# A Mamba block with a routed feed-forward: VectorE's multiplication by C moved behind the unit's first other operation

## The chip, the cores and the metric

The kernel runs on one core of one Trainium2 chip. The metric is the device time of one execution in microseconds (us), lower is better. A core has five engines that each run their own instruction queue in order: TensorE (PE), VectorE (DVE), ScalarE (ACT), GpSimd (POOL) and SyncE (SP, here only DMA issues). They wait for each other by semaphores.

## The reference, cut to what matters

Input are 16 rows of 512 positions by 256 features. Each row goes through two halves, each behind a layer norm that is modulated per row: a state space block and a feed-forward with 16 experts, of which each position uses 4.

```
xb = silu(conv3(xn @ W_in[:, :512]));  z = xn @ W_in[:, 512:]
dt = softplus(xb @ W_dt + b_dt);  B = xb @ W_B;  C = xb @ W_C        # 16 states
for t in positions:                                                   # 512 inner channels x 16 states
    h = exp(dt_t * A) * h + (dt_t * x_t) * B_t
    y_t = sum over states of h * C_t
x = x + ga * (residual + ((y + D * xb) * silu(z)) @ W_out)
x = x + gb * experts(layernorm(x) modulated)                          # sigmoid router, top 4 of 16
```

The multiplication by C that the change moves is `h * C_t` of the recurrence, for one state at a time.

## The kernel before

Channels lie on the 128 partitions, in 4 blocks of 128; two blocks make a pair. A **unit** is one state of one pair: 128 x 1024 values (two blocks of 512 positions). A row has 16 states times 2 pairs, 32 units, and the stretch in which a row's 32 units run is called its slot (`NU = 32`). There are 16 slots, so 512 units, and a short tail (`TAIL = 14`). Within a slot the first 6 units are states of pair 0 alone, then the pairs alternate (so two units in a row read the same row of C), and the last 6 are pair 1 alone.

For unit g the engines do this, each in its own queue:

- GpSimd: `drive` multiplies dt*x by B into a slot of the ring `unit` (five slots), two units ahead of VectorE.
- ScalarE: `decay` computes exp(dt * a) twice (one block each) into the PSUM buffer `hbank[g % 2]`. It waits for `c_scaled` of unit g - 2, that is, until the multiplication by C has read that buffer.
- VectorE: `scan` (L765) runs the recurrence in `hbank`. `times_c` (L778) multiplies it by C into the same ring slot, or straight into the sum `gsum` for a pair's first state, and increments `c_scaled`. It waits for the scan's own semaphore and for the row of C.
- GpSimd: `add` (L1375) issues a DMA that adds the ring slot to `gsum`, one unit later.
- SyncE: `load_b` and `load_c` fetch the rows of B and C three units ahead, into rings of four; `load_c` waits for `c_scaled` of the row's last reader.

Everything else is laid beside the units by a fixed plan. A unit has three moments (`part` 0, 1, 2), so a slot has 96. `streams` lists for each slot which work runs between which moments: the norm of the next row, its convolution and silu (VectorE L625, L628, L636), step sizes, gates (L644), the products y times gate (`mix`, L785), the projection of the row before, its statistics, its router (`pick`: six operations, then four, then the rest, L659 to L723) and weights. The experts of the row before run beside both (`Halves`, from moment 38 of a slot to moment 131, that is, into the next one): for each of 16 steps TensorE makes a gate and an up product (L509), ScalarE a tanh (L1103), VectorE two operations (L736, L743), GpSimd one (L1328), and TensorE the down product (L521); twice a row VectorE adds the result (L753, L756). TensorE's products other than `mbank` share three PSUM banks in strict turns. Each engine walks the same plan with its own lag (VectorE two moments, ScalarE one, GpSimd three), so the order of each queue is fixed when the program is written.

On VectorE the walk of a unit is: the scan; in part 0 the experts' step if one is due and then the streams; in part 1 `times_c`, then streams, then experts; in part 2 streams, then experts. Nothing is due in many parts.

Of the kernel before, what the change touches and what calls it, by code (L numbers as in the profile page):

```python
# [47 lines left out]
class Steps:  # L48
# [3 lines left out]
        self.gen, self.steps, self.first, self.final, self.done = gen, steps, first, final, 0  # L52

    def at(self, moment):
        if not self.first <= moment <= self.final:
            return
        upto = (moment - self.first + 1) * self.steps // (self.final - self.first + 1)
        while self.done < upto:
            next(self.gen, None)
            self.done += 1  # L60
        if moment == self.final:
            for _ in self.gen:
                pass


class Halves:
# [3 lines left out]
        self.gen, self.count, self.first, self.final, self.done = gen, count, first, final, 0  # L70

    def at(self, moment):
        while self.done < self.count and self.done * (self.final - self.first) < self.count * (moment - self.first):
            next(self.gen)
            self.done += 1

    def rest(self):
        while self.done < self.count:
            next(self.gen)
            self.done += 1  # L80


def build(nc, d, out):
# [3 lines left out]
    E, I, _ = d["L0_ffn_gate_proj"].shape  # L87
# [7 lines left out]
    NU = 2 * NS  # L95
# [11 lines left out]
    EP = E // 2  # L107
# [3 lines left out]
    ACT_LAG, DVE_LAG, POOL_LAG, SP_LAG = 1, 2, 3, 3  # L111
# [7 lines left out]
    with ctx:  # L119
# [126 lines left out]
        def x1_ready(need, row):  # L246

            for h in range(2):
                t = work.at["proj", row, h]
                need.wait_ge(t.free, t.after)  # L250
# [49 lines left out]
        def xb_at(row, q):  # L300

            return q + DK * (row % 2)
# [35 lines left out]
        def experts_at(older, young, moment):  # L338


            if older:
                older.at(moment + 3 * NU)
            if young:
                young.at(moment)

        def in_columns(dst, src):
            return dst[:, :], d["L0_attn_" + src].rearrange("(k p) -> p k", p=P)
# [269 lines left out]
        def _(eng):  # L617
            need = Passed(eng)

            def silu_inputs(row, pair):  # L620
                for q in (2 * pair, 2 * pair + 1):
                    t, n = work.at["conv", row, q], DK * row + q + 1
                    cv = conv[:, q % 2, :]
                    need.wait_ge(conv_act, n)
                    eng.scalar_tensor_tensor(out=cv[:, 1:T], in0=t.bank[:, 0:T - 1], scalar=conv_w[:, q, 0:1],  # L625
                                             in1=cv[:, 1:T], op0=ALU.mult, op1=ALU.add).then_inc(conv_v, 1)
                    need.wait_ge(conv_v, 2 * n - 1)
                    eng.scalar_tensor_tensor(out=cv[:, 0:T - 1], in0=t.bank[:, 1:T], scalar=conv_w[:, q, 2:3],  # L628
                                             in1=cv[:, 0:T - 1], op0=ALU.mult, op1=ALU.add).then_inc(conv_v, 1)
                    yield  # L630
                    yield
                    need.wait_ge(silu_act, n)
                    if row >= 2:
                        y = work.at["y", row - 2, q]
                        need.wait_ge(y.full, y.after)
                    eng.scalar_tensor_tensor(out=xb[:, xb_at(row, q), :], in0=t.bank[:, :], scalar=1.0, in1=cv, op0=ALU.add,  # L636
                                             op1=ALU.mult).then_inc(t.free, 1)
                    yield

            def gates(row):  # L640
                for q in range(DK):
                    t = work.at["gate", row, q]
                    need.wait_ge(gate_act, DK * row + q + 1)
                    eng.scalar_tensor_tensor(out=gz[:, q, :], in0=gz[:, q, :], scalar=1.0, in1=t.bank[:, :],  # L644
                                             op0=ALU.add, op1=ALU.mult).then_inc(t.free, 1)
                    yield
                    yield

            def pick(row):
# [30 lines left out]
                eng.tensor_reduce(r_g[:, :], r_two[:, :, :], AX.X, ALU.max).then_inc(route_v, 1)  # L680
                eng.tensor_reduce(g_bank, r_two[:, :, :], AX.X, ALU.max).then_inc(route_v, 1)
                at += 1
                yield

                g = r_g[:, :].rearrange("p (t g) -> p t g", g=NGRP)
                this = g.rearrange("p t (g a) -> p t g a", a=1).to_broadcast([P, TT, NGRP, NGRP])
# [13 lines left out]
                    scalar=1.5, in1=members.rearrange("p (t g) m -> p t g m", t=TT), op0=ALU.is_lt,  # L700
                    op1=ALU.mult).then_inc(t.free, 1)
                at -= 1
                yield

                need.wait_ge(t.free, t.after)
                for q in range(TT):
# [16 lines left out]
                eng.tensor_tensor(w_tok[:, :, :], r_w[:, :, 0:E], r_rec[:, :].rearrange(  # L723
                    "p (t a) -> p t a", a=1).to_broadcast([P, TT, E]), ALU.mult).then_inc(route_v, 1)
                assert at + 16 == ROUTE_V * (row + 1)
                yield

            def experts(row):
                for s in range(E + 1):
                    n = E * row + s  # L730
                    a = act[:, n % MOE_RING, :, :].rearrange("p j t -> p (j t)")
                    if s < E:

                        t = work.at["gates2", row, s]
                        need.wait_ge(etanhed, n + 1)
                        eng.scalar_tensor_tensor(out=a, in0=a, scalar=1.0, in1=t.bank[:, :], op0=ALU.add,  # L736
                                                 op1=ALU.mult).then_inc(t.free, 1)
                    yield
                    if s < E:
                        g, t = t, work.at["ups2", row, s]  # L740
                        need.wait_ge(t.full, t.after)
                        need.wait_ge(g.free, g.after)
                        eng.tensor_tensor(a, a, t.bank[:, :], ALU.mult).then_inc(t.free, 1)  # L743
                    yield
                    yield
                    if s in (EP, E):
                        h = s // EP - 1
                        tiles = slice(h * TT // 2, (h + 1) * TT // 2)
                        need.wait_ge(down_done, n)
                        need.wait_ge(gb_in, 16 * (row + 1))  # L750
                        x1_ready(need, row)
                        sums = mbank[:, :].rearrange("p (t h) -> p t h", h=H)
                        eng.tensor_tensor(sums, sums, gb_row[:, :].rearrange("p (a h) -> p a h", a=1).to_broadcast(  # L753
                            [P, TT // 2, H]), ALU.mult).then_inc(moe_v, 1)
                        need.wait_ge(moe_v, 2 * row + h + 1)
                        eng.tensor_tensor(xt[:, row % 2, tiles, :], sums, xt[:, row % 2, tiles, :],  # L756
                                          ALU.add).then_inc(moe_out, 1)
                    yield

            def scan(g):  # L760

                need.wait_ge(driven, g + 1)
                need.wait_ge(decayed, 2 * g + 2)
                h = hbank[g % HB][:, :, :].rearrange("p a t -> p (a t)")
                eng.tensor_tensor_scan(h, h, unit[:, g % RING, :, :].rearrange("p a t -> p (a t)"), 0.0, ALU.mult,  # L765
                                       ALU.add).then_inc(scanned, 1)
# [14 lines left out]
            def mix(row, pair):  # L781
                for q in (2 * pair, 2 * pair + 1):
                    t = work.at["y", row, q]
                    need.wait_ge(t.full, t.after)
                    eng.tensor_tensor(gz[:, q, :], gz[:, q, :], t.bank[:, :], ALU.mult).then_inc(t.free, 1)  # L785
                    yield
                    yield

            def turn_chunks():
                for n, (_, dst, split) in enumerate(chunks):  # L790
                    yield
                    t = work.at["turned", n, 1]
                    o = dst[:, 2:4, :].rearrange("p e h -> p (e h)") if split else dst[:, 2:4, :, :].rearrange(
                        "p e k i -> p (e k i)")
                    need.wait_ge(t.full, t.after)
                    eng.tensor_scalar(o, t.bank[:, :], 0.5 if split else 1.0, None, ALU.mult).then_inc(t.free, 1)
                    yield


            def first_norm():  # L800
# [94 lines left out]
            older = None  # L895
            for slot in range(NB + 1):
                run = slot < NB
                beside = streams(slot, stage_of) if run else last_streams(stage_of)
                young = experts_of(slot - 1, experts) if run else Halves(
                    experts(NB - 1), HALVES, *LAST_EXPERTS_AT)  # L900
                for k in range(NU if run else TAIL):
                    g = slot * NU + k
                    if run:
                        scan(g)
                    for part in range(3):
                        moment = 3 * k + part
                        if part == 0:
                            experts_at(older, young, moment - DVE_LAG)
                        if part == 1 and run:
                            times_c(g)  # L910
                        for s in beside:
                            s.at(moment - DVE_LAG)
                        if part:
                            experts_at(older, young, moment - DVE_LAG)
                older = young
            older.rest()

# [710 lines left out]
```

## Time and profile before

| | |
|---|---|
| median of 3 runs | 2645.66 us (2642.53 to 2646.27) |
| the profiled execution | 2637.64 us, its span 2635.9 us |
| busy: VectorE | 2385.8 us, 91% of the span |
| busy: TensorE (matmul) | 2303.2 us, 87% |
| busy: GpSimd | 2255.9 us, 86% |
| busy: ScalarE | 1489.0 us, 56% |
| first scan, last scan | 55.4 us, 2494.6 us |
| first scans of slots 5, 6, 7, 8 | 803.2, 958.2, 1112.0, 1265.9 us |
| granted TensorE clock | 0.949 of full speed |

Busy shares are averages over stages with different limits, so the rows below are by stage. An instruction's start may lie before the recorded end of the one ahead of it on the same engine: the engine has begun on it while the last results of the other are being written. What an operation takes of a full engine is therefore read from start to start. A bracket at a row's end is idle time of that engine directly before it, and what ended it.

### The profile page before, as it was taken

Reading aid. Unit: us, or ns where it says so; the run is one execution under the profiler, and the core shown is the slowest. Engines: PE = TensorE matmul, PEld = TensorE weight load, DVE = VectorE, ACT = ScalarE, POOL = GpSimd, SP = SyncE. Lnnn points to the kernel's source line nnn. Section 1 sums busy time; section 2 is a strip of 40 time slices with the busy share of each in tenths; the row PEclk is TensorE's granted clock in tenths of the full one; section 3 lists DMA queues with packets and bytes.
Section 4 is the critical chain, followed back from the end, with each engine's and each line's share of the span. In section 5 each row is a group of like instructions: output and inputs, shape, how many; then the busy total and the mean of one; then the engine's idle time right before and its main releaser. Section 6 shows DMA issues by size and latency. Waiting matters only on the chain.

```text
span 2635.9 us, 28145 instructions
## 1 busy us (share of the span) xinstructions
PE 2303.2 (87%) x8814; PEld 1648.3 (63%) x8814; DVE 2385.8 (91%) x2390; ACT 1489.0 (56%) x2825; POOL 2255.9 (86%) x1591
## 2 busy tenths in 40 slices
PE   6356998989989898998989899898989999898799
PEld 2224675756667576666757666575666667576678
DVE  4999999999999999999999999999999999999922
ACT  5656556565655656565565656556565665654320
POOL 2888999998999899899989998999889899988812
PEclk9677999999999999999999999999989999899899
DMA  6998999989999998989999898998989899898911
GB/s 167 256 218 209 216 224 215 235 207 243 214 219 222 210 243 200 248 215 219 222 206 248 192 246 211 224 224 207 249 193 235 209 229 233 200 249 192 233 49 48
DMA packets 312886, 558.72 MB, mean 212 GB/s; under 512 B 46864, under 2 KB 157456, under 8 KB 312736
## 3 DMA queue, kind: packets, MB, share of 16 engines
q0 software_dynamic: 77568, 260.08, 51.2%
q1 hardware_dynamic: 235168, 296.84, 36.9%
q8 instruction: 69, 1.13, 0.2%
q14 instruction: 81, 0.66, 0.1%
HBM read 295.10 MB, written 10.06 MB: 116 GB/s over the span
## 4 chain that ended last, share of the span: by engine, by line
PE 46%; POOL 20%; DVE 13%; issue 9%; ACT 7%; DMA 5%; SPq 0%; POOLq 0%; DVEq 0%
PE wbank L509 17%; PE mbank L521 9%; POOL unit L1361 8%; DVE hbank L765 7%; PE wbank L410 6%; DMA gsum<-unit 4%; PE wbank L451 4%; PE wbank L536 3%; POOL gsum L1375 3%; POOL act L1328 2%; ACT z L939 2%; POOL stat L1249 2%; ACT hbank L1133 2%; PE wbank L435 1%; PE wbank L471 1%
## 5 line engine op out<-in xcount | busy, mean ns | idle before, releaser
L1361 POOL TENSOR_TENSOR unit<-dtx,b_bc 128x1024 f32<-128x1024 f32 x512 | 1417.3, 2790 | 36.5 <-DVE dtx L842 27.9
L765 DVE TENSOR_TENSOR_SCAN hbank<-hbank,unit 128x1024 f32<-128x1024 f32 x512 | 1173.3, 2292 | 50.3 <-ACT hbank L1133 46.6
L1133 ACT ACTIVATE hbank<-dt,a_neg 128x512 f32<-128x512 f32 x1024 | 669.1, 681 | 241.9 <-DVE unit L778 240.0
L1375 POOL DMA_DIRECT2D gsum<-unit x480 | 560.2, 1167 | 73.1 <-DMA gsum<-unit 35.8
L778 DVE TENSOR_TENSOR unit<-hbank,c_bc 128x1024 f32<-128x1024 f32 x480 | 585.4, 1220 | 22.5
L521 PE MATMUL mbank<-down_t,act 128*128 128x256 f32 x2048 | 525.0, 394 | 27.0 <-POOL act L1328 25.9
L509 PE MATMUL wbank<-h_t,up_t 128*128 128x256 f32 x2048 | 509.9, 394 | 37.7 <-DVE xb L636 27.2
L1328 POOL TENSOR_TENSOR act<-act,w_all 128x512 f32<-128x512 f32 x256 | 410.0, 1602 | 142.0 <-DVE act L743 128.2
L509 PE MATMUL wbank<-h_t,gate_t 128*128 128x256 f32 x2048 | 487.3, 381 | 6.3 <-DVE xb L636 5.6
L521 PEld LDWEIGHTS mbank<-down_t,act 128*128 128x128 f32 x2048 | 398.7, 198 | 148.6 <-issue 51.5
L509 PEld LDWEIGHTS wbank<-h_t,up_t 128*128 128x128 f32 x2048 | 397.8, 197 | 141.3 <-DVE xb L636 38.8
L509 PEld LDWEIGHTS wbank<-h_t,gate_t 128*128 128x128 f32 x2048 | 388.0, 190 | 98.0 <-issue 39.0
L1103 ACT ACTIVATE act<-wbank 128x512 f32<-128x512 f32 x256 | 150.6, 588 | 311.4 <-PE wbank L509 311.2
L736 DVE SCALAR_TENSOR_TENSOR act<-act,wbank 128x512 f32<-128x512 f32 x256 | 173.8, 679 | 78.4 <-ACT act L1103 76.9
L410 PE MATMUL wbank<-xb,w_dt 128*128 128x512 f32 x496 | 227.1, 602 | 16.8 <-DVE xb L636 12.7
L743 DVE TENSOR_TENSOR act<-act,wbank 128x512 f32<-128x512 f32 x256 | 174.0, 680 | 13.8 <-PE wbank L509 8.4
L410 PEld LDWEIGHTS wbank<-xb,w_dt 128*128 128x128 f32 x496 | 95.2, 193 | 114.6 <-issue 106.4
L435 PE MATMUL wbank<-xn_t,w_in 128*128 128x512 f32 x256 | 139.9, 675 | 24.3 <-DVE gz L644 21.9
L398 PE MATMUL wbank<-xn_t,w_in 128*128 128x512 f32 x256 | 126.2, 620 | 24.7 <-DVE xb L636 18.1
L536 PE MATMUL wbank<-gsum,ident 128*128 128x512 f32 x256 | 123.8, 607 | 17.2 <-DMA gsum<-unit 17.2
L380 PE MATMUL wbank<-ident,z 128*128 128x128 f32 x256 | 42.4, 306 | 102.7 <-ACT z L939 90.7
L996 ACT ACTIVATE wbank<-z 128x512 f32<-128x512 f32 x60 | 36.1, 602 | 167.1 <-DVE z L628 167.1
(140 smaller groups left out, 2210.8 us busy)
## 6 DMA issues: line engine op xcount, KB each, us to landing
gsum<-unit POOLq DMA_DIRECT2D x480, 512.0 KB, 7.9
b_bc<-bc_scratch SPq DMA_DIRECT2D x352, 256.0 KB, 7.2
c_bc<-bc_scratch SPq DMA_DIRECT2D x352, 256.0 KB, 7.2
w_all<-w_scratch SPq DMA_DIRECT2D x256, 256.0 KB, 4.9
ht<-in_L_attn_x_dram SPq DMA_DIRECT2D x16, 512.0 KB, 6.1
w_out<-in_L_attn_W_out_dram SPq DMA_DIRECT2D x16, 512.0 KB, 8.0
ht<-in_L_attn_x_dram POOLq DMA_DIRECT2D x16, 512.0 KB, 8.0
out_dram<-xt SPq DMA_DIRECT2D x16, 512.0 KB, 3.1
```

What stands on the lines that cost most here:

```text
L410: m = eng.matmul(t.bank[:, :], w_dt[:, k, m_ * P:(m_ + 1) * P], xb[:, xb_at(row, k), :], start=k == 0, stop=k == DK - 1)
L509: m = eng.matmul(t.bank[:, j * HT:(j + 1) * HT], w[:, 2 * first + j, k, :], h2_t[:, row % 2, k, h * HT:(h + 1) * HT], start=k == 0, stop=k ...
L521: m = eng.matmul(mbank[:, u * H:(u + 1) * H], act[:, (n - 1) % MOE_RING, j, u * P:(u + 1) * P], down_t[:, e, :], start=(e == 0 and u == 0) ...
L536: m = eng.matmul(t.bank[:, :], ident[:, :], gsum[:, (2 * p + k) % SUMS, a, :], start=k == 1, stop=k == 0)
L736: eng.scalar_tensor_tensor(out=a, in0=a, scalar=1.0, in1=t.bank[:, :], op0=ALU.add, op1=ALU.mult).then_inc(t.free, 1)
L743: eng.tensor_tensor(a, a, t.bank[:, :], ALU.mult).then_inc(t.free, 1)
L765: eng.tensor_tensor_scan(h, h, unit[:, g % RING, :, :].rearrange("p a t -> p (a t)"), 0.0, ALU.mult, ALU.add).then_inc(scanned, 1)
L778: eng.tensor_tensor(o, hbank[g % HB][:, :, :], c_bc[:, s:s + 1, :].to_broadcast([P, 2, T]), ALU.mult).then_inc(c_scaled, 1)
L1133: eng.activation(hbank[g % HB][:, a, :], dt[:, 2 * q + a, :], ACT.Exp, scale=a_neg[:, 2 * q + a, n:n + 1]).then_inc(decayed, 1)
L1328: eng.tensor_tensor(a, a, w_all[:, n % W_RING, :, :], ALU.mult).then_inc(weighted, 1)
L1361: eng.tensor_tensor(unit[:, g % RING, :, :], dtx[:, 2 * q:2 * q + 2, :], b_bc[:, s:s + 1, :].to_broadcast([P, 2, T]), ALU.mult).then_inc(d ...
L1375: eng.dma_start(gsum[:, 2 * pair + k, :, :], unit[:, g % RING, :, :], accum_op=ALU.add).then_inc(summed[pair][k], 16)
```

## The change

Each step of a stream on VectorE now says how many operations it made, and the walk of a unit keeps `times_c` back until one was made, at the latest until the end of the unit. `times_c` stands behind the first part that made something. Where part 0 made something, the queue is as before; where nothing else is due in the unit, too. No operation is added or removed, and the other engines' queues are the same.

```diff
 class Steps:
     def at(self, moment):
+        made = 0
         if not self.first <= moment <= self.final:
-            return
+            return made
         upto = (moment - self.first + 1) * self.steps // (self.final - self.first + 1)
         while self.done < upto:
-            next(self.gen, None)
+            made += next(self.gen, None) or 0
             self.done += 1
         if moment == self.final:
-            for _ in self.gen:
-                pass
+            for more in self.gen:
+                made += more or 0
+        return made
...
@@ def experts (VectorE)
-                    yield
+                    yield int(s < E)
...
@@ the walk of a slot on VectorE
                     if run:
                         scan(g)
+                    due = run
                     for part in range(3):
-                        moment = 3 * k + part
+                        moment, made = 3 * k + part, 0
                         if part == 0:
-                            experts_at(older, young, moment - DVE_LAG)
-                        if part == 1 and run:
+                            made += experts_at(older, young, moment - DVE_LAG)
+                        for s in beside:
+                            made += s.at(moment - DVE_LAG)
+                        if part:
+                            made += experts_at(older, young, moment - DVE_LAG)
+                        if due and (made or part == 2):
                             times_c(g)
-                        for s in beside:
-                            s.at(moment - DVE_LAG)
-                        if part:
-                            experts_at(older, young, moment - DVE_LAG)
+                            due = False
```

The other yields of VectorE's streams change in the same way (`yield 2` behind the two convolution taps, `yield 1` behind a silu, gate, mix or copy, `yield 6`, `4` and `7` in `pick`, `2 * int(s in (EP, E))` behind the experts' sums), and `Halves.at` and `experts_at` pass the number on.

## Rows read from the trace of the kernel before

**Rows 1.** Busy time by window: us, PE, PEld, DVE, ACT, POOL, clock, DMA
```profile
996.00:1060.00 64.00, 50.03 (x202) 34.96 (x201) 60.18 (x76) 44.38 (x105) 59.33 (x46) 0.97 0.85 205
1060.00:1148.00 88.00, 88.00 (x339) 64.51 (x338) 85.59 (x73) 48.21 (x72) 80.52 (x54) 0.98 0.99 236
```

**Rows 2.** Timeline of TensorE: start us, us, engine, line, operation, shapes [idle before]
```profile
1059.54 3.48 PE L509 MATMUL wbank<-h_t,up_t 128*128 128x256 f32 x8 [1.95 <-DVE xb L636]
```

**Rows 3.** Timeline at the end of that stretch, ScalarE and VectorE
```profile
1149.75 0.38 ACT L1045 ACTIVATE xt<-wbank 128x256 f32<-128x256 f32 x1 [3.64 <-PE wbank L454]
...
1151.88 2.30 DVE L765 TENSOR_TENSOR_SCAN hbank<-hbank,unit 128x1024 f32<-128x1024 f32 x1 [1.09 <-ACT hbank L1133]
```

**Rows 4.** Timeline of VectorE, two units (k=25 and 26 of slot 6)
```profile
1079.95 2.29 DVE L765 TENSOR_TENSOR_SCAN hbank<-hbank,unit 128x1024 f32<-128x1024 f32 x1
1082.15 0.67 DVE L743 TENSOR_TENSOR act<-act,wbank 128x512 f32<-128x512 f32 x1
1082.74 1.21 DVE L778 TENSOR_TENSOR unit<-hbank,c_bc 128x1024 f32<-128x1024 f32 x1
1083.86 2.29 DVE L765 TENSOR_TENSOR_SCAN hbank<-hbank,unit 128x1024 f32<-128x1024 f32 x1
1086.26 1.23 DVE L778 TENSOR_TENSOR unit<-hbank,c_bc 128x1024 f32<-128x1024 f32 x1
1087.40 0.68 DVE L736 SCALAR_TENSOR_TENSOR act<-act,wbank 128x512 f32<-128x512 f32 x1
1088.18 0.69 DVE L743 TENSOR_TENSOR act<-act,wbank 128x512 f32<-128x512 f32 x1
```

**Rows 5.** Router at k=11: slot 6 (VectorE, ScalarE), slot 5, and its waits in all
```profile
1006.36 2.29 DVE L765 TENSOR_TENSOR_SCAN hbank<-hbank,unit 128x1024 f32<-128x1024 f32 x1
1008.68 1.23 DVE L778 TENSOR_TENSOR unit<-hbank,c_bc 128x1024 f32<-128x1024 f32 x1
1009.82 0.22 DVE L659 SCALAR_TENSOR_TENSOR r_ch<-wbank,choice_bias 128x64 f32<-128x64 f32 x1
...
1010.87 0.25 DVE L681 TENSOR_REDUCE wbank<-r_two 128x16 f32<-128x96 f32 x1
1011.15 0.23 DVE L690 TENSOR_TENSOR wbank<-wbank,r_g 128x64 f32<-128x64 f32 x1
...
1009.04 0.22 ACT L1084 ACTIVATE r_s<-wbank 128x64 f32<-128x64 f32 x1
...
855.92 0.23 DVE L659 SCALAR_TENSOR_TENSOR r_ch<-wbank,choice_bias 128x64 f32<-128x64 f32 x1 [1.02 <-ACT r_s L1084]
...
DVE r_ch L659 <- ACT r_s L1084: 9.6, 7, 3.3
```

**Rows 6.** GpSimd's sum behind k=12's multiplication: slot 6, slot 4
```profile
1020.01 0.93 POOL L1375 DMA_DIRECT2D gsum<-unit  x1 [0.28 <-DVE unit L778]
...
711.36 0.91 POOL L1375 DMA_DIRECT2D gsum<-unit  x1
```

**Rows 7.** The scan of k=17, slot 6
```profile
1038.68 2.30 DVE L765 TENSOR_TENSOR_SCAN hbank<-hbank,unit 128x1024 f32<-128x1024 f32 x1 [0.81 <-ACT hbank L1133]
```

**Rows 8.** The scan of k=15, slot 0
```profile
119.10 2.30 DVE L765 TENSOR_TENSOR_SCAN hbank<-hbank,unit 128x1024 f32<-128x1024 f32 x1 [1.70 <-ACT hbank L1133]
```

**Rows 9.** GpSimd's last sum, behind the last unit
```profile
2498.66 0.86 POOL L1375 DMA_DIRECT2D gsum<-unit  x1 [1.75 <-DVE unit L778]
```

**Rows 10.** Around k=3 of slot 7: VectorE, ScalarE, the scan of k=5
```profile
1124.22 2.29 DVE L765 TENSOR_TENSOR_SCAN hbank<-hbank,unit 128x1024 f32<-128x1024 f32 x1
1126.61 1.23 DVE L778 TENSOR_TENSOR unit<-hbank,c_bc 128x1024 f32<-128x1024 f32 x1
...
1127.32 0.60 ACT L1103 ACTIVATE act<-wbank 128x512 f32<-128x512 f32 x1 [3.60 <-PE wbank L509]
1127.82 2.52 ACT L1133 ACTIVATE hbank<-dt,a_neg 128x512 f32<-128x512 f32 x4
...
1133.73 2.29 DVE L765 TENSOR_TENSOR_SCAN hbank<-hbank,unit 128x1024 f32<-128x1024 f32 x1
```

More of the change, by code:

```diff
@@ L72, in at @@
     def at(self, moment):
+        made = 0
         while self.done < self.count and self.done * (self.final - self.first) < self.count * (moment - self.first):
-            next(self.gen)
+            made += next(self.gen) or 0
             self.done += 1
+        return made
     def rest(self):
@@ L338, in experts_at @@
         def experts_at(older, young, moment):
+            made = 0
             if older:
-                older.at(moment + 3 * NU)
+                made += older.at(moment + 3 * NU)
             if young:
-                young.at(moment)
+                made += young.at(moment)
+            return made
         def in_columns(dst, src):
@@ L629, in silu_inputs @@
                                              in1=cv[:, 0:T - 1], op0=ALU.mult, op1=ALU.add).then_inc(conv_v, 1)
-                    yield
+                    yield 2
                     yield
@@ L637, in silu_inputs @@
                                              op1=ALU.mult).then_inc(t.free, 1)
-                    yield
+                    yield 1
             def gates(row):
@@ L645, in gates @@
                                              op0=ALU.add, op1=ALU.mult).then_inc(t.free, 1)
-                    yield
+                    yield 1
                     yield
@@ L682, in pick @@
                 at += 1
-                yield
+                yield 6
                 g = r_g[:, :].rearrange("p (t g) -> p t g", g=NGRP)
@@ L702, in pick @@
                 at -= 1
-                yield
+                yield 4
                 need.wait_ge(t.free, t.after)
@@ L725, in pick @@
                 assert at + 16 == ROUTE_V * (row + 1)
-                yield
+                yield 7
             def experts(row):
@@ L737, in experts @@
                                                  op1=ALU.mult).then_inc(t.free, 1)
-                    yield
+                    yield int(s < E)
                     if s < E:
@@ L743, in experts @@
                         eng.tensor_tensor(a, a, t.bank[:, :], ALU.mult).then_inc(t.free, 1)
-                    yield
+                    yield int(s < E)
                     yield
@@ L757, in experts @@
                                           ALU.add).then_inc(moe_out, 1)
-                    yield
+                    yield 2 * int(s in (EP, E))
             def scan(g):
@@ L785, in mix @@
                     eng.tensor_tensor(gz[:, q, :], gz[:, q, :], t.bank[:, :], ALU.mult).then_inc(t.free, 1)
-                    yield
+                    yield 1
                     yield
@@ L796, in turn_chunks @@
                     eng.tensor_scalar(o, t.bank[:, :], 0.5 if split else 1.0, None, ALU.mult).then_inc(t.free, 1)
-                    yield
+                    yield 1
             def first_norm():
```

## The prediction

> **What bounds the kernel now.** The table of busy shares names no bound (VectorE 91%, TensorE 87%, GpSimd 86%), so I read by stage. One slot (a row's 32 units) lasts about 154 us, and slots 2 to 14, counted from 0, repeat each other closely; I use slot 6 and the start of slot 7 (1112.0), with k for a unit's place in its slot. The busy time by window splits 152 us in two: in the 64 us from k=9 to k=20 TensorE has 14 us idle, in the 88 us after them none, while VectorE is idle 2.4 us there [rows 1]. TensorE's timeline shows where that stretch starts, behind the convolution's last step on VectorE [rows 2]; at its end ScalarE waits 3.64 us for the projection, and the next scan 1.09 us for ScalarE [rows 3]. So from k=21 to k=8 of the next slot TensorE sets the pace; before that it is a chain through ScalarE, VectorE and GpSimd.
>
> **What VectorE gains.** I worked the plan's arithmetic (steps and halves by moment, lag 2) through for all 512 units. In 241 another operation stands ahead of the multiplication already, in 112 the unit has no other, and in 159 the multiplication moves: ten a slot in slots 2 to 14, at k=0, 1, 3, 5, 11, 13, 15, 24, 26, 31. The timeline prices it [rows 4]: an independent operation starts 2.20 us after its scan (1079.95 to 1082.15), the multiplication 2.40 us after it (1083.86 to 1086.26), and 2.32 where it is the second reader of its C row (1006.36 to 1008.68 in [rows 5]). An independent follower comes 0.59 us behind a 0.67 us operation, whether it is the multiplication (1082.15 to 1082.74) or not, and 1.12 to 1.14 us behind a multiplication. So a move saves 0.12 or, mostly, 0.19 to 0.20 us; over the 159 (50 and 109 times) that is 27 us. In 44 units it also comes between an expert's two operations, whose start-to-start is 0.78 us back to back (1087.40 to 1088.18) against 0.59: 8 us more. In all 35 us of VectorE time, 1.3%. The edit adds no instruction and no new pair of engines to wait on each other.
>
> [...]
>
> **Where the gain goes.** Seven of the ten places (24, 26, 31, 0, 1, 3, 5) lie in the stretch in which TensorE has no gap. What VectorE wins there becomes a longer wait for ScalarE ahead of the scan of k=9: worth 0. Places 13 and 15 lie between the multiplication of k=12 and the scan of k=17. There GpSimd runs without a gap from the sum it issues at 1020.01, waiting 0.28 us for the multiplication of k=12 [rows 6], through the norm of the next row, and the scan of k=17 then waits 0.81 us for ScalarE behind that [rows 7]. Also 0.
>
> **What the move costs.** At k=11 the first other operations are the router's six. They need ScalarE's scores, written from 1009.04 to 1009.26, while the scan is through for a follower at 1006.36 + 2.20 = 1008.56. Today the multiplication (1008.68 to 1009.82) covers that gap, and in other slots not all of it: the router's first operation waits in 7 cases, 9.6 us together, 1.02 of them in slot 5 [rows 5]. In the new order VectorE stands still until about 1009.30; the six go by, and the multiplication's 1.14 us comes behind them, less 0.11 as the pair 1010.87 to 1011.15 (0.28 apart) loses its dependent step (0.17): 1.03 us later if the scores already were the last to come. Here the router starts 0.52 us sooner than today, so 0.51 is left. The rest of the router, the scan of k=12 and its multiplication follow without a gap. Reading the same rows in 15 slots gives 0.51 to 0.69 us in seven (2, 3, 6, 7, 10, 14, 15) and 1.03 in eight.
>
> How much of it passes? GpSimd issues the sum 5.62 us after the scan of k=12 when VectorE is last; where its own chain is later the loss is covered. In the slots that start at 1.03, GpSimd is later by 1.13 us in slots 4, 11 and 12 (711.36 without a wait, [rows 6]), 1.0 in 8, 0.5 in 1 and 13, 0.1 in 5 and 0 in 9. With the six uncovered small ones of slots 2 to 14 (0.51, 0.54, 0.51, 0.63, 0.69, 0.51) the sum over slots 1 to 14 is 0.5 + 0.03 + 0.93 + 1.03 + 0.5 + 3.4 = 6.4 us. Behind it lie the scan of k=17 and a VectorE without a free place up to TensorE's restart, so it ends up in the span.
>
> The ends. Slot 0 has no experts. Moves at k=3, 4, 7, 8 and 11 save 0.9 us ahead of the wait at k=15 (1.70 us for ScalarE [rows 8]); ScalarE and GpSimd are paced by the multiplications there, so I take all of it, with bounds 0 and -1.4 (all eight moves). In slot 15 the router costs 0.5 and 13 and 15 give back 0.2 before GpSimd takes over. In the last unit of all the multiplication stands 0.39 us later (2.20 + 0.59 against 2.40), and GpSimd's last sum waits for it [rows 9]; k=26 gives 0.36 back. Together +0.3. Sum: 6.4 - 0.9 + 0.3 = +5.8 us.
>
> **The lateness itself.** Behind a moved multiplication wait ScalarE's two decays for the scan two units on, GpSimd's sum (and the slot of the ring behind it) and SyncE's load of a C row; nothing else is moved past a queue. The longest delay is k=3: the scan at 1124.22, then a mix and an expert's operation whose tanh ends at 1127.92, then the multiplication, at 1128.55 in place of 1126.61. Its signal comes about 1129.8; ScalarE's decays for k=5 then end near 1131.2 in place of 1130.3, and the scan that needs them starts at 1133.73 [rows 10]. Slack 2.5 us, cost 0; in the other places the delay is 0.4 to 1.8 us. If an activation fell in between, the bound is the 1.9 us of lateness in each of 13 slots: 25 us.
>
> **Result.** The profiled execution took 2637.64 us (span 2635.9), so 2643.4 is expected of it; the median of the runs shown is 8.0 us above it, and the same +5.8 there gives 2651.5. A measurement of this kernel tells about 0.2% (5.3 us) from no change, and the forecast sits on that edge. I call the likeliest case slower, with its own range +1 to +11: the low end has half the slots covered and slot 0 at its best, the high end has none covered (7 times about 0.57 and 8 times 1.03, 12 us).
>
> **Rivals.**
> - VectorE bounds throughout and the 35 us come back, less 12 us at the router: -23 us, about 2623. For it: in the first window VectorE is the busiest, 60.2 of 64 us [rows 1]. Against: TensorE has no gap for 88 us, and VectorE waits at its end. A weaker form, in which a third passes (-8), belongs here. Chance 0.12.
> - All absorbed: the router's scores often come later than shown, or GpSimd's chain does, and the cost hides as in slots 4, 8, 11 and 12: within 3 us. Chance 0.28.
> - The delayed multiplication reaches ScalarE's queue: a decay held by it stands ahead of an expert's tanh, TensorE gets its bank back late and loses its gapless stretch. It decides from 2.5 us of lateness at k=3; price 1 to 1.9 us in 13 slots: +13 to +25 on top, about 2670. Chance 0.10.
> - An operation between scan and multiplication saves VectorE nothing: the 0.9 us of slot 0, the 0.5 us of slot 15 and the 0.11 at each router fall away, so about +9 us, 2654. The pairs of 2.20 and 2.40 us [rows 4] leave it 0.02. [...]
>
> The forecast has 0.48, of which 0.28 lies above the edge and 0.20 below; of the absorbed case 0.02 is faster, the rest within. So faster 0.12 + 0.02 = 0.14, same 0.20 + 0.26 = 0.46, slower 0.28 + 0.10 + 0.02 = 0.40. The range takes in forecast and absorbed case, the weak form of the first rival and the start of the third: 2638 to 2663.
>
> **What the profile after would show.** In ten places a slot the multiplication starts 2.79 us or more after its scan; the idle time ahead of the router's first operation grows to some 0.7 us in every slot and up to 2.2 where it waits today; ahead of the scan of k=9 it grows from 1.09 by up to the 1.9 us won before it; from k=12 to k=17 nothing changes; slots like 6 get 0.5 us longer. I am wrong if the scan of k=9 no longer waits for ScalarE (VectorE was the bound), if TensorE shows idle time after k=22, or if the scan of k=5 begins to wait.

## The result and the profile after

The change makes the kernel slower by 0.42%: ratio of the times after to before 1.0042, 95% interval 1.0030 to 1.0054 (about 11 us). The medians of six runs each, 2653.57 and 2645.66 us, lie 7.9 us (0.30%) apart, at the low end of that interval. The profiled execution of the changed kernel has a span of 2651.8 us, 15.9 above the one before, which was 8.0 us faster than its kernel's median; so the two traces show more than the typical loss. All ratios compare executions in the chip's ordinary state: one of 7047.88 us (the added operation at k=12) and one of 3411.16 us (the kernel before) are outside it. The forecast was 2651.5 us and +0.22%: right in direction and in the place of the loss, and about half of the measured ratio.

The page after, its busy line and three of its groups (line engine op, operands, count | busy, mean ns | idle before, releaser). In the changed file the scan is L771, the multiplication by C L784, the decay L1141, the experts' first operation L742.

```profile
PE 2313.2 (87%) x8814; PEld 1660.8 (63%) x8814; DVE 2367.7 (89%) x2390; ACT 1492.9 (56%) x2825; POOL 2255.9 (85%) x1591
...
L771 DVE TENSOR_TENSOR_SCAN hbank<-hbank,unit 128x1024 f32<-128x1024 f32 x512 | 1172.9, 2291 | 41.6 <-ACT hbank L1141 39.1
L784 DVE TENSOR_TENSOR unit<-hbank,c_bc 128x1024 f32<-128x1024 f32 x480 | 583.7, 1216 | 10.9
L742 DVE SCALAR_TENSOR_TENSOR act<-act,wbank 128x512 f32<-128x512 f32 x256 | 174.1, 680 | 113.1 <-ACT act L1111 111.5
```

VectorE is busy 18 us less than before (2385.8). What it saved is found again as waiting: the experts' first operation now waits 111.5 us for ScalarE's tanh in all, where the page of before has 76.9:

```profile
L736 DVE SCALAR_TENSOR_TENSOR act<-act,wbank 128x512 f32<-128x512 f32 x256 | 173.8, 679 | 78.4 <-ACT act L1103 76.9
```

The rest of the saving is idle time: 22.5 us ahead of the multiplication became 10.9, and 13.8 ahead of the experts' second operation became 8.0. With the 18 us that makes 35.5, the 35 us of the prediction. Against it stand the 34.6 us more ahead of the experts' first operation and 8.7 less ahead of the scans (50.3 to 41.6), so about three quarters of the saving are found again in these two rows. The loss is in another row, VectorE's waits for the router's scores (engine, result, line, waited for: us in total, times, longest):

```profile
DVE r_ch L665 <- ACT r_s L1092: 34.0, 16, 3.5
```

It was 9.6 us in 7 cases [rows 5]. Here is the router at k=11 of slot 6, the timeline of VectorE (start us, us, ...), with ScalarE's scores and TensorE's logits beside it:

```profile
1011.95 2.29 DVE L771 TENSOR_TENSOR_SCAN hbank<-hbank,unit 128x1024 f32<-128x1024 f32 x1
1016.53 0.23 DVE L665 SCALAR_TENSOR_TENSOR r_ch<-wbank,choice_bias 128x64 f32<-128x64 f32 x1 [2.30 <-ACT r_s L1092]
...
1017.59 0.25 DVE L687 TENSOR_REDUCE wbank<-r_two 128x16 f32<-128x96 f32 x1
1017.75 1.21 DVE L784 TENSOR_TENSOR unit<-hbank,c_bc 128x1024 f32<-128x1024 f32 x1
1018.88 0.22 DVE L696 TENSOR_TENSOR wbank<-wbank,r_g 128x64 f32<-128x64 f32 x1
...
1016.28 0.22 ACT L1092 ACTIVATE r_s<-wbank 128x64 f32<-128x64 f32 x1
...
1012.43 3.57 PE L477 MATMUL wbank<-router_t,h_t 128*128 128x16 f32 x16 [1.50 <-ACT h_t L1081]
```

The order is the forecast one: the scan, six operations, the multiplication 0.16 us behind the sixth and 1.13 us wide. The wait is 2.30 us, not 0.7; over slots 2 to 15 it is 0.92 to 2.30. The scores came late, because the 16 small matrix products of the logits took 3.57 us, and the windows show why (us, then busy time by engine, granted clock, DMA):

```profile
1006.00:1011.00 5.00, 3.47 (x20) 2.63 (x18) 4.82 (x5) 4.58 (x10) 4.82 (x5) 1.00 0.64 141
1011.00:1013.00 2.00, 0.56 (x3) 0.60 (x4) 2.00 (x2) 1.29 (x2) 2.00 (x3) 0.78 0.28 84
1013.00:1017.00 4.00, 4.00 (x18) 3.82 (x18) 1.67 (x3) 0.93 (x3) 4.00 (x3) 0.50 0.95 237
```

TensorE had the full clock (2.4 GHz) until about 1012.1, was busy for only 0.56 of the 2 us from 1011 to 1013, and worked at half (1.2 GHz) through the logits. In slot 6 of the kernel before it was as idle ahead of the logits, and the clock fell as well, but only 1.8 us after their start, so that they took 1.93 us:

```profile
1005.00:1007.00 2.00, 0.51 (x6) 0.30 (x3) 1.90 (x3) 1.69 (x3) 2.00 (x3) 1.00 0.23 49
1007.00:1011.00 4.00, 4.00 (x21) 3.39 (x21) 3.86 (x8) 2.17 (x10) 4.00 (x3) 0.71 1.02 226
```

In other slots of the kernel before it fell earlier; there the multiplication stood in front of the router and part of the lateness hid behind it.

The start of every scan in the two traces, compared slot by slot, shows where the rest of a slot stands. Call lag what a scan of the changed kernel starts later than the same scan of the kernel before. From k=12 to k=17 of slot 6 the changed kernel's lag goes from 7.72 to 7.71 us, from k=17 to k=24 it stays at 7.71, up to k=9 of slot 7 it falls to 7.61, and from k=11 to k=12 it grows: by 2.13 us in slot 6, and by 0.3 to 2.1 in the others from 2 to 15.

### The profile page after: what moved, and what is told of

The parts are those of the page before. It is cut to its first block, busy times and chain, and to the rows that moved or that the text cites. A ratio compares the mean times of both kernels' runs of the same rounds, so it can differ in the third digit from the quotient of the medians.

```text
span 2651.8 us, 28145 instructions
## 1 busy us (share of the span) xinstructions
PE 2313.2 (87%) x8814; PEld 1660.8 (63%) x8814; DVE 2367.7 (89%) x2390; ACT 1492.9 (56%) x2825; POOL 2255.9 (85%) x1591
## 3 DMA queue, kind: packets, MB, share of 16 engines
q8 instruction: 69, 1.13, 0.2%
## 4 chain that ended last, share of the span: by engine, by line
PE 49%; POOL 17%; DVE 13%; issue 8%; ACT 7%; DMA 5%; SPq 0%; POOLq 0%; DVEq 0%
PE wbank L515 18%; PE mbank L527 9%; PE wbank L416 7%; POOL unit L1369 7%; DVE hbank L771 6%; PE wbank L457 4%; PE wbank L542 3%; POOL gsum L1383 2%; DMA gsum<-unit 2%; ACT z L947 2%; POOL act L1336 2%; PE wbank L477 2%; PE wbank L427 2%; POOL stat L1257 2%; DVE unit L784 2%
## 5 line engine op out<-in xcount | busy, mean ns | idle before, releaser
L771 DVE TENSOR_TENSOR_SCAN hbank<-hbank,unit 128x1024 f32<-128x1024 f32 x512 | 1172.9, 2291 | 41.6 <-ACT hbank L1141 39.1
L1141 ACT ACTIVATE hbank<-dt,a_neg 128x512 f32<-128x512 f32 x1024 | 671.7, 681 | 278.3 <-DVE unit L784 276.8
L784 DVE TENSOR_TENSOR unit<-hbank,c_bc 128x1024 f32<-128x1024 f32 x480 | 583.7, 1216 | 10.9
L515 PE MATMUL wbank<-h_t,gate_t 128*128 128x256 f32 x2048 | 488.4, 381 | 11.8 <-DVE xb L642 11.1
L742 DVE SCALAR_TENSOR_TENSOR act<-act,wbank 128x512 f32<-128x512 f32 x256 | 174.1, 680 | 113.1 <-ACT act L1111 111.5
```

The lines of the kernel that those rows point to most:

```text
L515: m = eng.matmul(t.bank[:, j * HT:(j + 1) * HT], w[:, 2 * first + j, k, :], h2_t[:, row % 2, k, h * HT:(h + 1) * HT], start=k == 0, stop=k ...
L784: eng.tensor_tensor(o, hbank[g % HB][:, :, :], c_bc[:, s:s + 1, :].to_broadcast([P, 2, T]), ALU.mult).then_inc(c_scaled, 1)
L1141: eng.activation(hbank[g % HB][:, a, :], dt[:, 2 * q + a, :], ACT.Exp, scale=a_neg[:, 2 * q + a, n:n + 1]).then_inc(decayed, 1)
```

## The experiments

### Which place costs: all but the router, and the router alone

The multiplication goes back directly behind the scan either at k=11 alone or everywhere else. The diff shows both conditions; each kernel has one of them.

```diff
                         if part == 0:
                             made += experts_at(older, young, moment - DVE_LAG)
+                        if part == 1 and due and (slot and k == 11):        # all_but_router
+                        if part == 1 and due and (not (slot and k == 11)):  # router_alone
+                            times_c(g)
+                            due = False
```

> The change at 144 of its 159 places; only in the units of k=11 (15 slots) does the multiplication by C stay directly behind the scan. My theory (the router's place alone costs, all the other places lie beside work that is late anyway): the time of the kernel before, ratio 0.998 to 1.001, at best 1 us from slot 0. The rival in which VectorE bounds the slots: the 144 places save it some 33 us, so ratio about 0.988. The rival in which the lateness of the multiplication at k=3 and the like reaches ScalarE's queue: ratio 1.003 or more, most of the change's loss still there. In the trace I expect the waits ahead of the scans of k=7 and k=9 to stand and the router's first operation to wait no more than in the kernel before.

Measured: ratio 0.9999 (0.9985 to 1.0012). The 144 other places are worth nothing that can be measured. In its trace, from 356 to 2364 us (13 slots' time, from early in slot 2 on), the two longest of VectorE's waits read (the edit shifts the line numbers: L742 is still the experts' first operation, L771 the scan):

```profile
DVE act L742 <- ACT act L1114: 38.9, 65, 1.4
DVE hbank L771 <- ACT hbank L1144: 31.4, 41, 1.1
```

The same two in that window of the kernel before:

```profile
DVE hbank L765 <- ACT hbank L1133: 38.1, 56, 1.4
...
DVE act L736 <- ACT act L1103: 7.0, 13, 0.6
```

The tanh was waited for 13 times, 7.0 us together. Now it is 65 times: at k=1, 3, 15 and 26 the experts' operation stands where the multiplication stood, comes up to its tanh too early and waits. Most of the saving at the scan is paid back at the next operation; the waits ahead of the scans became 6.7 us shorter.

> The kernel before with one place a slot changed: at k=11 of slots 1 to 15 the multiplication stands behind the router's first six operations. My theory: the whole loss of the change, ratio 1.003 to 1.006 (some +7 to +15 us), and the scan of k=12 comes at 5.6 us behind the scores in every slot. The rivals: VectorE-bound would give 1.004 as well here, so this run tells only the queue rival apart, which expects less than half of the loss (under 1.002).

Measured: ratio 1.0056 (1.0043 to 1.0069). One place of ten in a slot has the whole loss. In its trace the scan of k=12 comes 5.6 us behind the scores in each of slots 2 to 14 (for instance 17.15 and 11.55 us after the scan of k=9 in slot 3), as expected. The wait for the scores:

```profile
DVE r_ch L665 <- ACT r_s L1095: 29.4, 16, 3.3
```

Together the two settle the first question. VectorE isn't the bound at the 144 places (had it been, the ratio of the first would be near 0.988), and their later multiplications don't reach ScalarE's queue either.

### What a microsecond of VectorE costs in two places

One reduction that nobody waits for is added to the kernel before, in slots 2 to 14, ahead of the scan of k=30 or of k=12. It takes 1.12 us of VectorE from start to start.

```diff
                 for k in range(NU if run else TAIL):
                     g = slot * NU + k
+                    if 2 <= slot <= 14 and k == 30:   # op_at_router: k == 12
+                        need.wait_ge(step_w_in, 16 * len(STEP_LOADS))
+                        eng.tensor_reduce(probe[:, :], w_dt[:, 0:2, :].rearrange("p a t -> p (a t)"), AX.X, ALU.max)
                     if run:
                         scan(g)
```

> The kernel before plus one VectorE operation that nobody waits for (a reduction over 1024 values a partition, about 1.1 us) ahead of the scan of k=30 in slots 2 to 14, 13 in all. It prices a microsecond of VectorE in the stretch where TensorE has no gap. My theory: the waits ahead of the scans of k=4, 7 and 9 (0.2 + 0.4 + 1.1 us) swallow it, so 0 to +2 us, ratio 1.000 to 1.001. If VectorE bounds: 13 x 1.1 = +14 us, ratio 1.0055.

Measured: ratio 1.0035 (1.0021 to 1.0049), span 2646.5, so about +9 us where 0 to 2 were expected. This expectation failed. The timelines of both engines in slot 3 show where:

```profile
643.07 1.21 DVE L906 TENSOR_REDUCE probe<-w_dt 128x1 f32<-128x1024 f32 x1
644.19 2.29 DVE L766 TENSOR_TENSOR_SCAN hbank<-hbank,unit 128x1024 f32<-128x1024 f32 x1
646.39 0.68 DVE L737 SCALAR_TENSOR_TENSOR act<-act,wbank 128x512 f32<-128x512 f32 x1
...
644.99 1.89 PE L522 MATMUL mbank<-down_t,act 128*128 128x256 f32 x8
647.12 1.99 PE L510 MATMUL wbank<-h_t,gate_t 128*128 128x256 f32 x8 [0.24 <-DVE act L737]
```

TensorE's groups of eight follow at 1.73 us when nothing is missing. Here the next one starts 2.13 us after the last, because it needs the bank that L737 frees, and further on some 0.1 us is lost at three more places (in slot 3, unlike slot 5, another 0.4 at 658.05). From slot 2 to slot 3, of 1.12 us 0.76 was still there at k=9 (lag against the kernel before 3.60 us at k=28, 4.36 at k=9 of the next slot); over the 13 slots it is 0.2 to 1.0 each and 8.5 in all, the +9 us of the run. So TensorE's stretch without a gap had in the mean about 0.4 us of cover against VectorE, not the 1.7 us that I had added up from VectorE's own waits. An engine that never waits says that a faster partner brings nothing; it doesn't say how much slower the partner may get.

> The same operation ahead of the scan of k=12 in slots 2 to 14, behind the router. My theory: it passes except where GpSimd is later anyway (3 x 1.1, 1.0, 0.5 and 0.1 us of cover in slots 4, 11, 12, 8, 13 and 5), so 14 - 5 = about +9 us, ratio 1.0025 to 1.0045. If VectorE bounds everywhere: +14, the same as the run beside it. If GpSimd's norm chain alone sets the scan of k=17: 0.

Measured: ratio 1.0066 (1.0048 to 1.0084), span 2654.1. That is about 17 us (13 to 22 by the interval, from three executions): above the +9 expected, and not told apart from the operation's own 13 x 1.12 = 15 us. The direction agrees; that the place is dearer than the one in the stretch (+9) is likely, but the intervals touch. The cover is there in the trace: from k=12 to k=17 the lag against the kernel before falls by 1.0 to 1.1 us in slots 4, 8, 11 and 12 and by 0.4 in slot 13. What lies above the +9 came in elsewhere. The logits are one candidate, not shown to be it: this trace has 3.2 to 3.6 us for them in eight of slots 2 to 15, the one before in four.

### Holding TensorE's clock

The two idle gaps ahead of the logits are filled with matrix products whose results are overwritten at once. Four kernels: the one before, the changed one, the router alone, all but the router.

```diff
+            def warm(t):
+                for _ in range(3):
+                    eng.matmul(t.bank[:, 0:H], ident[:, :], w_in[:, 0, 0:H], start=True, stop=True)
...
                     t = fill(("h2", row, k))
+                    if k == 0:
+                        warm(t)
                     need.wait_ge(rnormed, row + 1)
...
                 t = fill(("logits", row))
+                warm(t)
                 need.wait_ge(h2.free, h2.after)
```

> The kernel before with six more matrix products a row whose results are overwritten: three of 128x256 ahead of TensorE's wait for the second norm (it stands idle 1.45 us there) and three ahead of the router's logits (idle 1.49 us). In the traces so far the logits take 1.93 us at full clock and 2.1 to 3.57 us in slots where the granted clock falls to half behind these two gaps. My theory: with the gaps filled the clock stays, the logits take 1.93 us or less in (nearly) all slots, and the 0.9 us by which slots 4, 5, 8, 9, 11, 12 and 13 are longer than 153.8 us goes away: -5 to -12 us, ratio 0.9955 to 0.998. If the low clock has another cause than these gaps: 1.000 or a little more, logits as before.

Measured: ratio 0.9972 (0.9963 to 0.9981), median 2634.93 us. This is faster than both kernels. The groups of the logits by line, first of the kernel before, then of this one (idle before them at the end):

```profile
L471 PE MATMUL wbank<-router_t,h_t 128*128 128x16 f32 x256 | 41.2, 306 | 22.0 <-ACT h_t L1073 21.9
```

```profile
L478 PE MATMUL wbank<-router_t,h_t 128*128 128x16 f32 x256 | 31.1, 263 | 2.4 <-ACT h_t L1080 2.4
```

The idle time ahead of them falls from 22.0 to 2.4 us and they take 31.1 us instead of 41.2. In slots 2 to 15 the scores now end 11.12 to 11.13 us after the scan of k=9, each time; before, it was 11.18 to 12.82. Where they had been at 11.18 the products bring nothing else: the scan of k=12 starts at 16.30 in both traces.

> The changed kernel with the same six products. My theory: the scores then come at the same time in every slot, the router's place costs its smallest price (0.5 us) in slots 2 to 15, so this is 6 to 8 us above warm_before, ratio to the kernel before 0.998 to 1.001, and clearly below the changed kernel (1.0042). If the low clock had no share in the change's loss: 1.004 as the changed kernel.

Measured: ratio to the kernel before 0.9997 (0.9987 to 1.0008), median 2640.97, 6.0 us above warm_before. VectorE's timeline in slot 6:

```profile
1009.42 2.29 DVE L778 TENSOR_TENSOR_SCAN hbank<-hbank,unit 128x1024 f32<-128x1024 f32 x1
1012.29 0.22 DVE L672 SCALAR_TENSOR_TENSOR r_ch<-wbank,choice_bias 128x64 f32<-128x64 f32 x1 [0.58 <-ACT r_s L1099]
...
1013.34 0.25 DVE L694 TENSOR_REDUCE wbank<-r_two 128x16 f32<-128x96 f32 x1
1013.50 1.22 DVE L791 TENSOR_TENSOR unit<-hbank,c_bc 128x1024 f32<-128x1024 f32 x1
1014.62 0.22 DVE L703 TENSOR_TENSOR wbank<-wbank,r_g 128x64 f32<-128x64 f32 x1
...
1017.85 2.29 DVE L778 TENSOR_TENSOR_SCAN hbank<-hbank,unit 128x1024 f32<-128x1024 f32 x1
```

This is the unit as the prediction drew it: a short wait, six operations, the multiplication, and the scan of k=12 at 8.43 us behind the one of k=11. In warm_before it comes 8.02 us behind (1005.56 to 1013.58). So the place costs 0.41 to 0.44 us with the clock held, where 0.51 was forecast, in each of slots 2 to 14: 5.4 of the 6.0 us. In slot 15 the scan of k=12 comes 17.90 us after the one of k=9 in both traces; a later operation of the router is shorter there by the same amount. The rest is less tidy: slots 0 and 1 bring 2.6 us in this pair of traces, and 2.4 us go again in other places.

> The router's place alone with the six products: the same as warm_after within 0.15%, 6 to 8 us above warm_before, ratio to the kernel before 0.998 to 1.001. If the other 144 places win time once the clock no longer falls (VectorE as the bound then): warm_after would be below this run by up to 33 us.

Measured: ratio to the kernel before 0.9998 (0.9989 to 1.0007), median 2641.83: the same as warm_after.

> The change without the router's place, with the six products: the fastest of the four. My theory: warm_before less 0 to 1 us, ratio to the kernel before 0.995 to 0.998. If VectorE is the bound once the clock stays: below warm_before by more than 0.3%.

Measured: ratio to the kernel before 0.9972 (0.9963 to 0.9982), median 2635.11: the same as warm_before, not faster. With the clock held as well, the 144 places bring nothing.

## Why the prediction came out as it did

**What bounds the kernel: right, with a blemish.** The stretch in which TensorE has no gap [rows 1] is there after the change too, but for one gap of 1.11 us at k=22, ahead of 1073.80, where it waits for the convolution's last step. By the sign that I had set (idle time of TensorE after k=22) this comes close to a refutation. It isn't one: the trace of before has the same gap in slots 4, 8, 10, 11 and 12, which slot 6 alone didn't show me, and the one of after has it in nine of slots 2 to 14. From 1074 to 1155 TensorE is busy 81.00 of 81 us:

```profile
1068.00:1155.00 87.00, 85.89 (x334) 62.23 (x333) 83.95 (x72) 48.00 (x72) 79.81 (x54) 1.00 0.98 236
1074.00:1155.00 81.00, 81.00 (x316) 58.99 (x316) 77.98 (x66) 44.66 (x66) 73.81 (x51) 1.00 0.98 237
```

**The saving and its loss: right in sum, wrong in one detail.** The pairs of 2.20 and 2.40 us hold, VectorE is busy 18 us less, and the saving buys nothing: 0.9999 and, with the clock held, no difference between 0.9972 and 0.9972. (The Trainium skill, VectorE: DVE Perf Modes, The DRAIN you can't avoid, says that a next operation that is not held starts before the pipeline has emptied. These pairs agree: the independent one starts 2.20 us after a scan of 2.29 us, the one that waits for its result 2.40 us after it.) The rival that an operation between saves VectorE nothing is refused by the busy time. But I expected it to pile up ahead of the scan of k=9, where 1.09 us are waited [rows 3]. That wait stayed at 1.10. The saving was spent earlier, by the experts' operations that now reach their tanh too soon (VectorE, slot 7):

```profile
1125.97 0.69 DVE L742 SCALAR_TENSOR_TENSOR act<-act,wbank 128x512 f32<-128x512 f32 x1 [0.38 <-ACT act L1111]
...
1135.57 0.69 DVE L742 SCALAR_TENSOR_TENSOR act<-act,wbank 128x512 f32<-128x512 f32 x1 [1.07 <-ACT act L1111]
...
1159.49 2.30 DVE L771 TENSOR_TENSOR_SCAN hbank<-hbank,unit 128x1024 f32<-128x1024 f32 x1 [1.10 <-ACT hbank L1141]
```

**The router: right in mechanism, half of the size.** The first operation's wait, the multiplication behind the sixth, its 1.03 us where the scores were already last: with the scores at 12.81 us in both traces (slot 5), the scan of k=12 comes at 17.42 before and 18.41 after, 0.99 us. The mis-sized term is the lateness of the scores. I took each slot's from the one profile of before (mean 11.80 us behind the scan of k=9 over slots 2 to 15). In the profile after, the mean is 12.48, and the logits took 50.7 us in all instead of 41.2:

```profile
L477 PE MATMUL wbank<-router_t,h_t 128*128 128x16 f32 x256 | 50.7, 346 | 22.0 <-ACT h_t L1081 21.9
```

Between k=11 and k=12 of slots 2 to 14 the lag grows by 18.3 us in all, before GpSimd's cover. With the scores of the trace before, the place would have made 10.1 of them (0.48 to 1.00 a slot, where 0.51 to 1.03 was forecast); the other 8.2 are scores that came later still. Where the multiplication had covered up to half a microsecond of lateness, each further tenth now goes to the scan of k=12. So one row's term became two: the place itself, 6.0 us with the clock held, and the lateness. With the clock free the change costs 0.42%, the router alone 0.56%; with it held 6 to 7 us, 0.25%. That the +5.8 us of the forecast lie so near the 6.0 us with the clock held is in part luck: 1.03 us a slot in half of the slots, less GpSimd's cover, happens to sum to what 0.41 us a slot does.

**The cover at k=12: mostly right.** The loss got smaller from k=12 to k=17 where the cover was read [rows 6] in slots 4, 8, 12 and 13: lag 5.27 to 4.17 us, 9.97 to 8.99, and by 1.1 and 0.4 us (read: 1.13, 1.0, 1.13, 0.5). In slot 11 it did so by only 0.2 of 1.13, and in slot 1, read with 0.5, and slot 10, without cover, it grew by 0.7.

**Slot 0: wrong.** The 0.9 us were there at k=12 (lag -0.94 us), and gone at k=13 (-0.01) and k=15 (+0.57): VectorE waited 1.58 and 0.77 us for gates that TensorE gave later. The router alone, whose queues in slot 0 are those of the kernel before, also got 1.5 us later between k=12 and k=13. In every other trace of this case, too, the scan of k=13 in slot 0 is later against this one than the scan of k=12 was, by 0.4 to 1.8 us. Slot 0 says nothing at this size.

**The lateness at k=3: right.** No scan at k=5 waits; nothing came back from ScalarE's queue. The price of VectorE's time in the stretch was misread when I expected 0 to 2 us for the added operation; the prediction itself needs only that a faster VectorE brings nothing there.

**What stays open.** Why the scores are later. Three kernels with the router unit stretched (after, the router alone, the added operation at k=12) have mean score times near 12.2 to 12.5 us, and three without (before, all but the router, the operation at k=30) near 11.6 to 11.8, one trace each. The granted clock of the executions goes the same way: in the mean it is 0.9447 for after (6 executions), 0.9446 for the router alone (5) and 0.9397 for the operation at k=12 (3), beside 0.9470 for the kernel before (16, measured with the last two) and 0.9465 for all but the router (12); the operation at k=30 (4) lies between with 0.9455.

The traces show a part of the way. The clock falls in every one of slots 2 to 15, in both kernels; what differs is when. The fall against the start of the logits (us, minus is before it), read off the granted clock:

| slot | 2 | 3 | 4 | 5 | 6 | 7 | 8 | 9 | 10 | 11 | 12 | 13 | 14 | 15 |
|---|---|---|---|---|---|---|---|---|---|---|---|---|---|---|
| before | 1.9 | 1.7 | 1.1 | -0.2 | 1.8 | 1.7 | 0.9 | -0.5 | 1.6 | 1.1 | -0.8 | 0.3 | 2.3 | 2.0 |
| after | 0.2 | 1.5 | 0.7 | -1.0 | -0.3 | 0.9 | -0.4 | 0.8 | -0.8 | -0.3 | -0.4 | 0.8 | -0.8 | 0.3 |

The logits take 1.93 us where the fall comes 1.8 us or more after their start, and 3.57 where it comes ahead of it. From slot 2 to slot 5 of the kernel before the falls follow each other at 153.6 us, the logits at 153.8, 154.2 and 154.9: a slot that got longer brings the next logits nearer to the fall or behind it, until the fall comes late again (slot 6). So the lateness of one slot does carry over to the next. That longer slots must on average be later ones, and that this makes up the other half of the loss, isn't shown. Held clocks take the effect away but don't tell its cause.

## What to carry to other kernels

Before an operation goes in front of another to hide a short dependence, ask what its own inputs wait for: the one that was moved back here was also the cover of a wait on a chain that sets the slot: without it the wait is 0.6 to 2.3 us, and it had hidden 0.6 to 1.3 of them. A term read from one trace is an average over slots; if a clock or a late partner makes it vary, the piece that loses its cover pays the whole variation. And the 0.2 us saved on an engine whose partner never stands still were for the most part found again in a wait one row further down.

## What the runs showed of the hardware

In slot 6 of the changed kernel TensorE's granted clock fell to half 0.3 us ahead of the logits, between two waits of 1.5 us, while it was busy 0.56 of 2 us, and the logits took 3.57 instead of 1.93 us. In slot 6 of the kernel before, with the same two waits, it fell 1.8 us behind the start of the logits, when TensorE was busy again: idle time and the price for it can lie apart, and who pays is what runs when the clock falls. Six products of 128x256 in these gaps, whose results nobody reads, kept the clock at 1.00 through the logits of slots 2 to 15 in all four traces that have them (it next fell 7.5 us or more after the start of the logits), and took 0.28% off a kernel that was otherwise unchanged.

An operation on VectorE that doesn't need the result of a scan of 2.29 us starts 2.20 us after it, one that waits for it after 2.40 us; among operations of 0.68 us it is 0.59 against 0.78 us. With 159 multiplications moved behind such an operation its busy time went from 2385.8 to 2367.7 us.
